# A recurrence's first operands loaded and split within the stage before it

## The reference

```python
w = jnp.exp(-jnp.exp(w)).reshape(B, L, H, S)          # decay
r = (xr @ Wr.T).reshape(B, L, H, S)                   # receptance
k = (xk @ Wk.T).reshape(B, L, H, S)
v = (xv @ Wv.T).reshape(B, L, H, S)
g = jax.nn.silu(xg @ Wg.T)                            # gate
def step(s, inp):
    k_l, v_l, w_l, r_l = inp
    a = k_l[..., :, None] * v_l[..., None, :]
    out = jnp.einsum('bhs,bhst->bht', r_l, faaaa * a + s)
    return (a + w_l[..., None] * s, out)
_, outs = jax.lax.scan(step, s0, seq)                 # 100 steps, state of 16 x 16 for each of 32 heads
```

## Time and profile before

| what | us |
|---|---|
| median of 3 runs | 2793.92 (2788.14 to 2794.48) |
| the profiled execution, by its own time | 2796.03 |
| span of the profile | 2794.3 |
| TensorE busy | 2504.8 (90%) |
| VectorE busy | 1397.7 (50%) |
| ScalarE busy | 1140.4 (41%) |
| GpSimd busy | 1112.1 (40%) |
| mean granted clock of TensorE | 0.941 of full |

### The profile page before, as it was taken

One profiled execution on the slowest core, in us unless ns is written; L12 is line 12 of the kernel. 1 busy time (PEld: TensorE's weight loads), 2 busy tenths in 40 slices (PEclk: granted clock), 3 DMA queues, 4 the chain that ended last, 5 costly groups with the idle time before them and its releaser, 6 DMA issues. The chain is left out here.

```text
span 2794.3 us, 37817 instructions
## 1 busy us (share of the span) xinstructions
PE 2504.8 (90%) x14008; PEld 2190.1 (78%) x14008; DVE 1397.7 (50%) x2347; ACT 1140.4 (41%) x2439; POOL 1112.1 (40%) x494
## 2 busy tenths in 40 slices
PE   7888489779998788899979999998998999999698
PEld 5665334468895555689969999988997899999698
DVE  4666621278885531223345566643334466665643
ACT  3776111222323211122356566641235566665321
POOL 1100322141111110162168879755323878877300
PEclk9999669989998889999989999998998999999899
DMA  7552601489992014062854445425275544442300
GB/s 228 120 124 70 221 24 40 143 213 239 239 226 92 1 61 149 22 209 101 276 169 155 144 153 167 146 62 175 114 240 184 163 152 135 154 150 93 117 31 24
DMA packets 215850, 385.68 MB, mean 138 GB/s; under 512 B 88740, under 2 KB 127676, under 8 KB 215028
## 3 DMA queue, kind: packets, MB, share of 16 engines
q1 hardware_dynamic: 215668, 383.28, 44.3%
HBM read 288.03 MB, written 103.35 MB: 140 GB/s over the span
## 5 line engine op out<-in xcount | busy, mean ns | idle before, releaser
L1732 PE MATMUL att_ring<-ca_pp,att_arena 128*128 128x400 f32 (+1 forms) x2304 | 438.5, 349 | 27.0 <-POOL att_arena L1814 16.8
L1732 PEld LDWEIGHTS att_ring<-ca_pp,att_arena 128*128 128x128 f32 (+1 forms) x2304 | 423.0, 191 | 36.5 <-POOL att_arena L1814 22.5
L1803 POOL TENSOR_TENSOR att_arena<-att_arena 128x1448 fp32r<-128x1448 f32 x64 | 212.1, 3313 | 254.6 <-ACT att_arena L1820 254.6
L1732 PE MATMUL att_ring<-att_arena,qk_wh 128*128 128x362 f32 x1024 | 256.8, 332 | 0.0
L2416 DVE TENSOR_TENSOR ca_yl<-att_ring,att_arena 128x400 fp32r<-128x400 f32 x256 | 146.7, 573 | 204.8 <-ACT att_arena L2375 204.8
L1814 POOL TENSOR_TENSOR att_arena<-state_X,att_arena 128x1536 fp32r<-128x1536 f32 x64 | 224.3, 3505 | 5.0
L1732 PE MATMUL rec_fbank<-rec_fch,rec_fwl 128*128 128x362 f32 x512 | 174.9, 342 | 24.9 <-POOL rec_fwl L1031 16.0
L1811 POOL TENSOR_TENSOR att_arena<-state_X,att_nothing 128x1536 fp32r<-128x1536 f32 x64 | 175.9, 2749 | 49.5 <-DMA state_X<-in_ctx 49.5
L1732 PE MATMUL att_ring<-att_arena,qk_wl 128*128 128x362 f32 x512 | 173.4, 339 | 18.5 <-POOL att_arena L1997 18.1
L1732 PEld LDWEIGHTS att_ring<-att_arena,qk_wh 128*128 128x128 f32 x1024 | 186.0, 193 | 0.0
L1732 PE MATMUL rec_fbank<-rec_fcl,rec_fwh 128*128 128x362 f32 x512 | 170.7, 333 | 0.0
(11 more groups left out here) (379 smaller groups left out, 5874.0 us busy)
## 6 DMA issues: line engine op xcount, KB each, us to landing
att_arena<-keys SPq DMA_DIRECT2D x64, 724.0 KB, 5.3
state_X<-in_ctx SPq DMA_DIRECT2D x64, 512.0 KB, 3.9
rec_vb<-kept_value SPq DMA_DIRECT2D x256, 100.0 KB, 5.3
queries<-att_arena SPq DMA_DIRECT2D x16, 1600.0 KB
att_arena<-queries SPq DMA_DIRECT2D x64, 400.0 KB
keys<-rec_stage SPq DMA_DIRECT2D x32, 724.0 KB, 4.2
keys<-att_kstage SPq DMA_DIRECT2D x32, 724.0 KB, 3.3
state_X<-in_ctx SPq DMA_DIRECT2D x64, 210.0 KB, 4.1
```

Source lines behind the costliest of these rows:

```text
L1732: issued = nc.tensor.matmul(out, x, y, start=(first and k == 0), stop=(last and k == count - 1))
L1803: self.nc.gpsimd.tensor_tensor(self.kl[:, n % 2].bitcast(F32R), self.kl[:, n % 2], self.kh[:, n % 2].bitcast(F32), ALU.subtract).then_inc( ...
```

## The change

Parts of what the recurrence loads and splits at its start are done in the gate stage:

- A new object `Ahead` is made before the stages. It holds an arena (the space of `cur` and `diff`, later of `dev` and `sq`), whose first half and more serves as the recurrence's `vb[0]`, `vb[1]`, `kb`, `rb`, `now` and `s0`, and new tiles of their own for the first weights and context (`fwh0`, `fwl0`, `fch0`, `fcl0`) and the raw weights of group 1 (`fwl1`).
- In the gate stage SyncE loads the first weights and context by chunks, group 1's weights, then, once they are stored, the values of batches 0 and 1, key, first state and receptance of b = 0, before it waits for `present`; and it waits for all of them at its end. ScalarE rounds a chunk of weights and of context behind each of the Silu slots 2 to 5; GpSimd subtracts all eight.
- In the recurrence these loads and splits are gone. SyncE begins with the decay of b = 0, the columns, group 2's weights, values of batch 2, group 3's weights, `present`, the next context, and the operands of b = 1. The first four units run in the normal order, head by head. TensorE waits for groups 1 to 3 chunk by chunk and not for all four chunks of a group. VectorE's first steps are rank1(0), scan(0), rank1(1), multiply(0), rank1(2), scan(1).
- Semaphores are divided to fit: one each for key, values and receptance kept; decay and receptance of the recurrence apart. `grow` becomes a view of `mix[1]`, and `low`, `lowg`, `lowd` are allocated after the layer norm.

The diff, cut to these parts:

```diff
+class Ahead:
+
+    def __init__(self, sc):
+        self.arena = sc.sb("arena", [P, 2 * B * CC * L])
+        self.fwh, self.fwl = sc.sb("fwh0", [P, CC, W3], F32R), sc.sb("fwl0", [P, CC, W3])
+        self.fch, self.fcl = sc.sb("fch0", [P, CC, SP], F32R), sc.sb("fcl0", [P, CC, SP])
+        self.next_weights = sc.sb("fwl1", [P, CC, W3])
+        self.place = 0
+        self.vb = [self.piece(4 * CC * L).rearrange("p (j c l) -> p j c l", j=4, c=CC) for _ in range(2)]
+        self.kb = self.piece(2 * CC * L).rearrange("p (i c l) -> p i c l", i=2, c=CC)
+        self.rb = self.piece(2 * CC * L).rearrange("p (i c l) -> p i c l", i=2, c=CC)
+        self.now = self.piece(2 * CC * L).rearrange("p (i c l) -> p i c l", i=2, c=CC)
+        self.s0 = self.piece(2 * HD * CC).rearrange("p (i j c) -> p i j c", i=2, j=HD)
+
+    def piece(self, count):
+        self.place += count
+        return self.arena[:, self.place - count:self.place]
+
+
+def spread_value(nc, value, dst, m, arrived):
+
+    rows = value[m // 4, :, m % 4 * 4:(m % 4 + 1) * 4, :].rearrange("h (a j) n -> h a (j n)", a=1)
+    for h in range(HEADS_CHUNK):
+        nc.sync.dma_start(dst[h * HD:(h + 1) * HD].rearrange("s j c l -> s (j c l)"),
+                          rows[h].broadcast_to([HD, 4 * CC * L])).then_inc(arrived, 16)
...
-        kb, rb, now = (sc.sb(n, [P, 2, CC, L]) for n in ("kb", "rb", "now"))
+        kb, rb, now, s0 = ahead.kb, ahead.rb, ahead.now, ahead.s0
         wb = sc.sb("wb", [P, 2, JB, N])
-        s0 = sc.sb("s0", [P, 2, HD, CC])
-        vb = sc.sb("vb", [P, RING_V, JB, CC, L])
+        vb = ahead.vb + [sc.sb(f"vb{i}", [P, JB, CC, L]) for i in range(2, RING_V)]
         work = [sc.sb(f"work{i}", [P, JB * N]) for i in range(RING_W)]
-        fwh, fwl = sc.sb("fwh", [P, GROUPS, CC, W3], F32R), sc.sb("fwl", [P, GROUPS, CC, W3])
-        fch, fcl = sc.sb("fch", [P, 2, CC, SP], F32R), sc.sb("fcl", [P, 2, CC, SP])
+        fwh = [ahead.fwh] + [sc.sb(f"fwh{g}", [P, CC, W3], F32R) for g in range(1, GROUPS)]
+        fwl = [ahead.fwl, ahead.next_weights] + [sc.sb(f"fwl{g}", [P, CC, W3]) for g in range(2, GROUPS)]
+        fch, fcl = [ahead.fch, sc.sb("fch1", [P, CC, SP], F32R)], [ahead.fcl, sc.sb("fcl1", [P, CC, SP])]
...
-            if i < G3 * CC:
-                return i % G3, i // G3
             return i // CC, i % CC
...
-            for c in range(CC):
-                sp.dma_start(fwl[:, 0, c], fills[0][0][:, c]).then_inc(first_weight_in[c], 16)
-                sp.dma_start(fcl[:, 0, c], ctxT[0][:, c]).then_inc(first_ctx_in[c], 16)
-                if c == 0:
-                    load_key(0)
-                if c == 1:
-                    load_values(0)
-            load_rest(0)
+            load_decay(0)
             for i in range(len(head_columns)):
                 sp.dma_start(columns[:, i], head_columns[i]).then_inc(columns_in, 16)
-            load_weights(1)
-            load_values(1)
             load_weights(2)
+            load_values(2)
+            load_weights(3)
+            sp.dma_start(now[:, 0], present[:, 0]).then_inc(now_in[0], 16)
+            load_context(1)
             load_key(1)
             load_rest(1)
-            load_weights(3)
-            load_context(1)
-            load_values(2)
             for tile, src in later:
...
             def high_weights(g):
-                act.wait_ge(fweight_in[g], 16)
-                nc.scalar.activation(fwh[:, g], fwl[:, g], ACT.Copy).then_inc(fweight_high, 1)
+                if g > 1:
+                    act.wait_ge(fweight_in[g], 16)
+                nc.scalar.activation(fwh[g][:], fwl[g][:], ACT.Copy).then_inc(fweight_high, 1)
...
-            for c in range(CC):
-                act.wait_ge(first_weight_in[c], 16)
-                nc.scalar.activation(fwh[:, 0, c], fwl[:, 0, c], ACT.Copy).then_inc(first_weight_high, 1)
-                act.wait_ge(first_ctx_in[c], 16)
-                nc.scalar.activation(fch[:, 0, c], fcl[:, 0, c], ACT.Copy).then_inc(first_ctx_high, 1)
             high_weights(1)
             act.wait_ge(columns_in, 16 * len(head_columns))
...
-                if u < G3 and h == 0:
-                    pe.wait_ge(first_weight_low, c + 1)
-                    pe.wait_ge(fctx_low, c + 1)
-                if u >= G3 and c == 0:
-                    if b == 0 and h == 0:
-                        pe.wait_ge(fweight_low, CC * g)
-                    if g == 0 and h == 0:
-                        pe.wait_ge(fctx_low, CC * (b + 1))
+                if b == 0 and g and h == 0:
+                    pe.wait_ge(fweight_low, CC * (g - 1) + c + 1)
+                if c == 0 and u >= RING_F:
+                    if b and g == 0 and h == 0:
+                        pe.wait_ge(fctx_low, CC * b)
                     pe.wait_ge(fill_kept, u - RING_F + 1)
...
-            for c in range(CC):
-                low_context(0, c)
...
-                dve.wait_ge(values_in[m % RING_V], 16 * HEADS_CHUNK * (m // RING_V + 1))
-                if q == 0:
-                    dve.wait_ge(key_in[b % 2], 32 * (b // 2 + 1))
+                if m > 1:
+                    dve.wait_ge(values_in[m % RING_V], 16 * HEADS_CHUNK * (m // RING_V + (m % RING_V > 1)))
+                if q == 0 and b:
+                    dve.wait_ge(key_in[b % 2], 32 * (b // 2 + b % 2))
...
-            for c in range(CC):
-                low_weights(c)
             rank1(0)
-            for m in range(BATCHES):
+            scan(0)
+            rank1(1)
+            multiply(0)
+            for m in range(1, BATCHES):
                 if m + 1 < BATCHES:
                     rank1(m + 1)
-                if m:
+                if m > 1:
                     multiply(m - 1)
                 scan(m)
...
+                if 2 <= u < 2 + CC:
+                    c = u - 2
+                    act.wait_ge(ahead_weight_in[c], 16)
+                    nc.scalar.activation(ahead.fwh[:, c], ahead.fwl[:, c], ACT.Copy).then_inc(ahead_weight_high, 1)
+                    act.wait_ge(ahead_ctx_in[c], 16)
+                    nc.scalar.activation(ahead.fch[:, c], ahead.fcl[:, c], ACT.Copy).then_inc(ahead_ctx_high, 1)
+
+        @block.gpsimd
+        def _(pool):
+            for c in range(CC):
+                pool.wait_ge(ahead_weight_high, c + 1)
+                nc.gpsimd.tensor_tensor(ahead.fwl[:, c].bitcast(F32R), ahead.fwl[:, c], ahead.fwh[:, c].bitcast(F32), ALU.subtract)
+                pool.wait_ge(ahead_ctx_high, c + 1)
+                nc.gpsimd.tensor_tensor(ahead.fcl[:, c].bitcast(F32R), ahead.fcl[:, c], ahead.fch[:, c].bitcast(F32), ALU.subtract)
 
         @block.sync
         def _(sp):
+            for c in range(CC):
+                sp.dma_start(ahead.fwl[:, c], by_chunks(fill_weights[0])[:, c]).then_inc(ahead_weight_in[c], 16)
+                sp.dma_start(ahead.fcl[:, c], fill_ctx[0][:, c]).then_inc(ahead_ctx_in[c], 16)
+            sp.dma_start(ahead.next_weights[:], by_chunks(fill_weights[1])).then_inc(next_weight_in, 16)
+            sp.wait_ge(values_kept, 16 * value_copies)
+            for m in range(2):
+                spread_value(nc, a["kept_value"], ahead.vb[m], m, first_values_in)
+            sp.wait_ge(key_kept, 16)
+            sp.dma_start(ahead.kb[:, 0], a["kept_key"][:, 0]).then_inc(first_key_in, 16)
+            sp.dma_start(ahead.s0[:, 0], a["first"][0]).then_inc(first_state_in, 16)
+            sp.wait_ge(receive_kept, 16)
+            sp.dma_start(ahead.rb[:, 0], a["kept_receive"][:, 0]).then_inc(first_receive_in, 16)
             a["kept_present"] = nc.dram_tensor("kept_present", tuple(ruk.shape), F32).ap()
             sp.wait_ge(now_done, B)
...
             sp.dma_start(a["kept_present"], ruk[:]).then_inc(kept, 16)
+            sp.wait_ge(next_weight_in, 16)
+            sp.wait_ge(first_values_in, 2 * 16 * HEADS_CHUNK)
+            sp.wait_ge(first_key_in, 16)
+            sp.wait_ge(first_state_in, 16)
+            sp.wait_ge(first_receive_in, 16)
...
+        ahead = Ahead(sc)
+        halves = [ahead.arena[:, i * NT * CC:(i + 1) * NT * CC].rearrange("p (b c l) -> p b c l", b=B, c=CC) for i in range(2)]
...
-            low, lowg, lowd = st.sb("low", [P, B, L]), st.sb("lowg", [32, B, L]), st.sb("lowd", [64, B, L])
-            cur, diff = st.sb("cur", big), st.sb("diff", big)
+            cur, diff = halves
...
-            grow = st.sb("grow", [P, 2, 4, L])
+            grow = mix[1][:, 0:2]
...
-            keep_in_dram(nc, "key", key, a, kept)
+            keep_in_dram(nc, "key", key, a, key_kept)
             mix_and_product(nc, "l1s", mixing(3, mix[0]), (CC, dense(W["WvT"], mix[1]), keep(value)))
-            value_copies = keep_values(nc, value, a, kept)
+            value_copies = keep_values(nc, value, a, values_kept)
...
-            keep_in_dram(nc, "receive", receive, a, kept)
+            keep_in_dram(nc, "receive", receive, a, receive_kept)
             await_copies(nc, (blocks_in, 1))
```

(8 more changed lines are left out.)

75 lines of the change are left out of this document (38 added, 37 removed).

## The result

The changed kernel takes 2768.82 us (median, 2767.36 to 2769.4) against 2793.72 for the kernel before on the same chip: a ratio of 0.9909 with a 95% interval of 0.9892 to 0.9925, 24.9 us less. The profiled execution took 2768.3 us. The forecast was 2767, with 2757 to 2780 as its range.

A forecast was written before the change was run, and what follows sets the result against it. TensorE bounds the steady part, so what counts is its gaps in the recurrence's opening (25.6 us); b = 1 starting at 583.3 instead of 610.0 saves 26.7 us off the 2793.92 median: 2767 us, range 2757 to 2780.

The forecast's parts named there:

- The gate stage is full and covers its transfers: Gate stage: added splits and queued transfers fit idle time; function-table switches taken as zero, 4 us in all at worst.
- The slip of 0.8 and the first fill at +29.04: Gate stage's end slips 0 to 1.6 us, taken as 0.8; first fill at 537.5 us, 4.0 us earlier.
- slower: Rival, chance 0.04: at 113 GB/s the gate stage's transfers end it 35.6 us late; 8.9 us slower, 2803 us.
- Group 1's 13.92 us become 1.3: Recurrence's opening: with group 1's weights already loaded, TensorE's wait for their low parts falls from 13.92 to 1.3 us.
- The first gather at +43.0: Opening: decay issued first lets VectorE finish for the first gather at 551.5 us; TensorE's wait there falls from 6.67 to 0.7.
- Group 2 at 0 to 1 us: Opening: groups 2 and 3 rounded 8 us ahead of need, so TensorE waits 0 to 1 us.
- The values of batch 3 at +54.8, the gap of 7.5: Before the second gather: queued values of batch 3 land at 563.3 us, gather at 567.9, a new 7.5 us TensorE gap.
- Three full waits for GpSimd: VectorE before the second gather, by the Trainium skill: 7.7 us for the 4.6 taken, making the time 3 us higher.
- The sum: Opening's total: b = 1 starts at 583.3 us against 610.0, 26.7 us less; the 252 us behind it unchanged.
- the values are not late: Rival, chance 0.14: queue moves values at 383 GB/s, no gap before the second gather; 33.4 us less, 2760.5 us.
- the gap only moves: Rival, chance 0.04: another wait replaces group 1's and that before the first gather; 8 us less at most, 2786 or higher.
- everything slow beside the spreads: Rival, chance 0.08: all transfers move at 202 GB/s, gate stage ends 7 us late; 8.6 us less, 2785.3 us.

The follow-up runs named there:

- group_waits: Changed kernel with TensorE waiting for all four low pieces of a group again, not chunk by chunk: stretch 325.4 us, median 2762.67 us, ratio 0.9893.

## Why the prediction was right, point by point

Times with a plus are from the gate stage's first product (508.46 before, 511.17 after).

**The gate stage is full and covers its transfers: right.** ScalarE still idles ahead of its slots with the splits between them, and loads no table between Silu and Copy, so of the two ends of that cost (0 and 4 us) it was 0. GpSimd's pieces of 1.27 and 0.95 us end at 536.24, ahead of the stage's end:

```profile
528.93 0.50 ACT L1160 ACTIVATE l_gate<-l1v_prod 128x400 f32<-128x400 f32 x1 [2.62 <-PE l1v_prod L1140]
529.34 0.62 ACT L1164 ACTIVATE l_fwh<-l_fwl 128x512 fp32r<-128x512 f32 x1
529.86 0.49 ACT L1166 ACTIVATE l_fch<-l_fcl 128x362 fp32r<-128x362 f32 x1
...
538.34 0.50 ACT L1160 ACTIVATE l_gate<-l1v_prod 128x400 f32<-128x400 f32 x1 [2.18 <-PE l1v_prod L1140]
```

**The slip of 0.8 and the first fill at +29.04: right, +29.2.** SyncE waits 1.0 us for `present`, and its first issue stands 1.45 us behind the last Silu where 0.5 is the ordinary distance. The rival "slower", a stage over 27 us late, was 26 us off. Two spreads in flight had moved only 147 to 163 GB/s in the gate stage, less than my 202, but the weights beside them 397 to 403, and the sum came out.

**Group 1's 13.92 us become 1.3: they became 0.** Its four pieces took 5.02 us from 542.29, and none was held up: the scan came only at 546.02, when `decay` had landed, together with the last piece, and here it was the scan that took longer (4.63 us for 3.48). **The first gather at +43.0: +43.06**, without a wait where I had 0.7; TensorE was late itself, at a granted clock of 0.65 in the stretch of 542 to 546 us, which was 1.2 GHz for most of it. The sum had that only behind the long gap.

**Group 2 at 0 to 1 us: mis-sized, 2.85 (2.38 and 0.47).** The term was "8 us ahead of need against 5.2 us of subtractions and 3.2 more where a scan comes between". It left out ScalarE's rounding itself, 1.92 us inside those 8, and counted one hold by VectorE where there were more; TensorE waited for the third and the fourth piece:

```profile
552.69 16.08 POOL L1040 TENSOR_TENSOR rec_fwl<-rec_fwl,rec_fwh 128x512 fp32r<-128x512 f32 x8 [5.38 <-ACT rec_fwh L972]
571.34 10.91 POOL L1044 TENSOR_TENSOR rec_fcl<-rec_fcl,rec_fch 128x362 fp32r<-128x362 f32 x4 [2.57 <-ACT rec_fch L978]
```

Eight pieces whose median is 1.28 us took 16.08, one of them 4.52; beside them VectorE ran products of 2.54 and 2.93 us for 1.77 to 1.81 and a copy of 1.27 for 0.17, and beside the context's pieces a scan of 4.23 for 3.48. That both sides stretch is what the Trainium skill says of two inputs from SBUF beside a reading GpSimd ("SBUF — State Buffer", Who interferes with whom), and it doesn't except the scan; the 4.52 us for one piece is 3.24 over the median, and it began at 558.08, together with a scan of 3.48 (558.07).

**The values of batch 3 at +54.8, the gap of 7.5: the mechanism right, the numbers near.** They landed at +56.3 and the gather stood at +61.1 for +59.4. From product to gather it was 4.8 us for my 4.6, so of the 1.7 us late 1.5 are the queue's. Three full waits for GpSimd, 7.7 us in the prediction, did not come: only the product was stretched. The gap was 5.66, since TensorE too came 3.5 us late, by the 2.85 in group 2 and by the lower clock. VectorE's timeline:

```profile
546.02 4.63 DVE L1075 TENSOR_TENSOR_SCAN rec_work<-rec_wb,rec_work 128x1600 f32<-128x1600 f32 x1 [3.79 <-DMA rec_wb<-kept_decay]
...
554.43 2.54 DVE L1066 TENSOR_TENSOR rec_work<-rec_vb,l_arena 128x1584 f32<-128x1584 f32 x1 [0.26 <-DMA rec_vb<-kept_value]
556.89 1.27 DVE L1067 COPY rec_work<-l_arena 128x16 f32<-128x16 f32 x1
...
567.50 2.93 DVE L1066 TENSOR_TENSOR rec_work<-l_arena 128x1584 f32<-128x1584 f32 x1 [5.95 <-DMA l_arena<-kept_value]
570.36 0.17 DVE L1067 COPY rec_work<-l_arena 128x16 f32<-128x16 f32 x1
570.43 1.81 DVE L1085 TENSOR_TENSOR rec_work<-rec_work,l_arena 128x1600 f32<-128x1600 f32 x1
```

**The sum: b = 1 begins at +76.3 for +74.8**, against +101.5 before, a gain of 25.2; 1.2 more came in the 252 us behind it, which I had left as they are. Together 26.4 for 26.7. That this is so close is partly luck, since errors cancel: group 1 and the first gather's wait were 2 us too dear, the lower clock behind the start was left out and cost about as much, and group 2's 2.85 us are hidden in the wait for the values. So the closeness of the sum is better than that of its terms.

**What the prediction missed.** It held the queue for the one limit behind the edit, so "the values are not late" was priced at 33.4 us less. The experiments price that case: with the values early the stretch is no shorter than with the change (3.1 longer in its one profile), and only with GpSimd's chain cut too it is 3.9 shorter, some 30 us under before. The rival "the gap only moves" was right for that next step, though not for the change. The rival "everything slow beside the spreads" is refuted by 292 GB/s in the gate stage. One reading in the prediction is wrong: of the some 358 GB/s that the Trainium skill gives as the limit from HBM to a core ("DMA: Bandwidth & Descriptors", Specifications) it says that the trace contradicts it both ways. Only the 383, and the 397 to 403 of the gate stage, do; a pace of 202 lies under a limit.

**Open:** what holds the spreads at some 200 GB/s; the order of the heads and the rows read from are excluded as its main cause, the pace of issue doesn't fit, the sixteen partitions of a single transfer are untested. Also the 1.2 us in the steady part, where TensorE has no gap in either kernel and a batch takes 8.92 to 8.98 us for 8.99 to 9.00, and the part of the whole time that isn't the stretch (26.4 in it, 24.9 in the medians), which lies within the run-to-run differences named above. No kernel tried is clearly better than the changed one: group_waits has the shortest stretch of those that do all of the computation, by 2.1 us, of which 0.8 lies ahead of the first fill.

## What to carry to other kernels

Work moved ahead under a covered stage is worth the wait that it removes as long as each engine's slack in that stage, and the queue's, is summed by bytes at the pace of the tiles that move, not at one bandwidth. After the first limit is removed, price the next engine's chain too, with its pieces stretched as beside a busy VectorE (here 2 us for 1.28): where TensorE waits for GpSimd, GpSimd for ScalarE and ScalarE for TensorE, a delay of one can come back to it. To judge an edit of a few us in a long kernel, measure from a mark ahead of the edit to one behind it, and take repeats of the same kernel as the yardstick; one profile of each version says little under 2 us.

## What the runs showed that was not expected

A transfer whose source has eight outermost rows ran at 117 GB/s with the engines 0.4 to 0.5 busy, where eight separate transfers of the same bytes move at 147 to 202 with all engines busy. Spreads from one row of memory or from sixteen different rows go about equally fast (packet 0.544 and 0.530 us, 0.533 in the repeat of the changed kernel), and so with the heads in another order. Last, one small delay is dear: 2.7 us of data (group 1's weights) put 9.4 us on the stretch, and a scan moved behind a product 9.2 in its one profile.
